# A causal mask folded into the contraction of the decays' matmul, and one projection block moved between its halves

## The reference

```
proj = x @ W_in.T;  gate, (x, B, C), dt = split(proj)
x, B, C = silu(causal_conv4(x, B, C) + conv_b)
dt = softplus(dt + dt_bias);  a = cumsum(dt * A)        # in chunks
L[l, s] = exp(a[l] - a[s]) for s <= l, else 0           # per head
Y = ((C B^T) * L) @ (x * dt)  +  exp(a) * C @ state  +  D * x
state = decay * state + (B * decay * dt)^T @ x
out = rmsnorm_by_group(Y * silu(gate)) * norm_weight @ W_out.T
```

## Time and profile before

| | us |
|---|---|
| median of 3 runs | 3062.11 (3061.02 to 3063.52) |
| profiled execution | 3058.52 |
| its span, first to last instruction | 3056.8 |
| PE busy / DVE / ACT / POOL | 2694.2 / 2116.4 / 1210.2 / 1138.0 |

### The profile page before, as it was taken

How to read it: one execution, slowest core, us unless ns; L and a number is a source line. 1 busy time by engine, 2 the same in 40 slices (tenths; PEclk the granted TensorE clock), 3 DMA queues, 4 the chain that set the end, 5 groups by cost and what they waited for, 6 DMA issues and landing times. The chain is left out here.

```text
span 3056.8 us, 44174 instructions
## 1 busy us (share of the span) xinstructions
PE 2694.2 (88%) x14212; PEld 1934.6 (63%) x14212; DVE 2116.4 (69%) x3433; ACT 1210.2 (40%) x2468; POOL 1138.0 (37%) x1240
## 2 busy tenths in 40 slices
PE   4893399999999999999999993699999959999993
PEld 2782277777777777777777772588888743333332
DVE  3466788888888888888888865677777765444434
ACT  1121255555555545545545541122222234444441
POOL 0350155464555545555455450355455400000000
PEclk9996599999999999999999996799999979999997
DMA  3100200000000000000000001100000031111114
GB/s 114 40 16 29 66 2 2 26 2 26 2 2 26 2 26 2 26 2 2 26 2 3 2 2 55 29 24 29 23 23 29 6 109 36 37 36 38 38 27 93
DMA packets 79209, 82.76 MB, mean 27 GB/s; under 512 B 22043, under 2 KB 67894, under 8 KB 76748
## 3 DMA queue, kind: packets, MB, share of 16 engines
q1 hardware_dynamic: 77516, 80.59, 8.9%
q10 hardware_dynamic: 1536, 0.20, 0.0%
HBM read 61.53 MB, written 16.78 MB: 26 GB/s over the span
## 5 line engine op out<-in xcount | busy, mean ns | idle before, releaser
L731 DVE SCALAR_TENSOR_TENSOR mix_cv<-mix_pp,mix_cw,mix_cv 128x384 f32<-128x384 f32 (+4 forms) x864 | 494.1, 572 | 90.7 <-ACT mix_cv L653 67.6
L1492 DVE TENSOR_REDUCE att_tops<-att_psc 128x1 f32<-128x512 f32 (+3 forms) x384 | 202.2, 555 | 217.9 <-PE att_psc L1430 131.7
L962 POOL TENSOR_TENSOR ffn_hl<-ffn_h,ffn_hh 128x512 fp32r<-128x512 f32 x144 | 186.2, 1293 | 319.8 <-ACT ffn_hh L1020 319.8
L653 ACT ACTIVATE mix_cv<-mix_pp,mix_cb,mix_cw 128x384 f32<-128x384 f32 (+1 forms) x288 | 182.0, 632 | 307.3 <-PE mix_pp L77 305.8
L1467 PE MATMUL att_po<-att_pr,att_vh 128*17 128x512 f32 (+3 forms) x768 | 290.6, 489 | 0.0
L577 PEld LDWEIGHTS mix_pyd<-mix_xdt,mix_lm 128*128 128x128 f32 x2048 | 247.4, 192 | 55.0 <-issue 53.1
L519 POOL TENSOR_TENSOR mix_xdt<-mix_xtok,l_dt 128x512 f32<-128x512 f32 x128 | 133.7, 1044 | 379.0 <-ACT mix_xtok L680 379.0
L1531 ACT ACTIVATE att_pr<-att_pst 128x512 f32<-128x512 f32 (+3 forms) x384 | 175.6, 489 | 249.5 <-PE att_pst L1449 246.0
L75 PE MATMUL mix_pp<-l0in_XH,mix_wx_lo 128*128 128x384 f32 (+2 forms) x576 | 231.0, 401 | 30.9 <-DVE mix_ss L720 21.7
L628 PE MATMUL mix_pgt<-mix_wo,mix_gt 128*128 128x256 f32 x1024 | 251.9, 390 | 2.9 <-issue 2.2
L577 PE MATMUL mix_pyd<-mix_xdt,mix_lm 128*128 128x64 f32 x2048 | 242.7, 272 | 0.9 <-DVE mix_lm L781 0.9
(11 more groups left out here) (296 smaller groups left out, 6753.6 us busy)
## 6 DMA issues: line engine op xcount, KB each, us to landing
mix_w_raw<-in_w_in SPq DMA_DIRECT2D x8, 1280.0 KB, 5.5
ffn_raw<-in_wgu SPq DMA_DIRECT2D x56, 128.0 KB, 2.2
mix_ll<-cs SPq DMA_DIRECT2D x384, 2.0 KB
att_qs<-q SPq DMA_DIRECT2D x192, 32.0 KB
mix_wo_raw<-in_w_out SPq DMA_DIRECT2D x8, 512.0 KB, 7.5
ffn_draw<-in_wd SPq DMA_DIRECT2D x28, 128.0 KB, 2.1
q<-qkv_part SPq DMA_DIRECT2D x24, 128.0 KB, 1.9
k<-qkv_part SPq DMA_DIRECT2D x24, 128.0 KB, 1.9
```

Source lines behind the costliest of these rows:

```text
L653: act.activation(conv_tile(k), pp[k % 2][:, halo:cols], ACT.Identity, bias=cb[:, it // 2, ct:ct + 1], scale=cw[:, it // 2, ct, 3:4]).then_ ...
L731: last = dve.scalar_tensor_tensor(out, of, cw[:, g, ct, 3 - d:4 - d], out, ALU.mult, ALU.add)
L962: pool.tensor_tensor(hl[u % NH][:, :], h[u % 2][:, :], hh[u % NH][:, :].bitcast(F32), ALU.subtract).then_inc(lo_done, 1)
L1492: dve.tensor_reduce(tops[o][:, col:col + 1], psc[g % 2][:, 0:end - c], AX.X, ALU.max).then_inc(mx_done, 1)
```

## The change

The mask becomes part of the first matmul. `ll` and `rl` grow from 27 rows to 96: rows 27 to 31 are zero, and rows 32 to 95 are 64 mask rows. Row 32+r of `rl` has -3e38 at the columns l with l % 64 = r in every head; row 32+r of `ll` has, for token half f, a one where s > r + 64 f. As 64 rows serve only 64 values of l, a half of the decays is done in two matmuls, for l below 64 and from 64 on, each with its own stationary operand (`ll` has now two copies of the a rows beside two sets of mask rows) and 4 x 64 = 256 columns, which are four runs of 64 in `rl` and in `pd`. Both have start and stop set. `identb`, `maskb`, their two casts and the mask's load are gone. The loads of `ll` write each row twice.

In the slot, the last fill now stands ahead of `decays(c, 1)`, not behind it. The other engines' orders stay.

```
-        rl = [s.sb(f"rl{j}", [27, GH, Q], BF16) for j in range(2)]
-        ll = [s.sb(f"ll{j}", [27, Q], BF16) for j in range(2)]
-        maskb, identb = s.sb("maskb", [P, 4 * Q], BF16), s.sb("identb", [P, P], BF16)
+        rl = [s.sb(f"rl{j}", [KD_ROWS, GH, Q], BF16) for j in range(2)]      # KD_ROWS = 32 + 64
+        ll = [s.sb(f"ll{j}", [KD_ROWS, 2, Q], BF16) for j in range(2)]
...
-                        sp.dma_start(ll[c % 2][3 + i * GH:3 + (i + 1) * GH, :],
-                                     cs3[i, g * GH:(g + 1) * GH, at]).then_inc(cs_in[c % 2], 16)
+                        sp.dma_start(ll[c % 2][3 + i * GH:3 + (i + 1) * GH, :, :],
+                                     cs3[i, g * GH:(g + 1) * GH, at].unsqueeze(1).to_broadcast([GH, 2, Q])).then_inc(cs_in[c % 2], 16)
...
-                    pe.matmul(pd[:, :], ll[o][:, :], rl[o][:, 4 * i:4 * i + 4, :], start=True, stop=False)
-                    pe.matmul(pd[:, :], identb[:, :], maskb[:, :], start=False, stop=True).then_inc(d_done, 1)
+                    for f in range(2):
+                        at = slice(f * HQ, (f + 1) * HQ)                     # HQ = 64
+                        last = pe.matmul(pd[:, :].rearrange("p (h q) -> p h q", h=4)[:, :, at], ll[o][:, f, :],
+                                         rl[o][:, 4 * i:4 * i + 4, at], start=True, stop=True)
+                    last.then_inc(d_done, 1)
...
+                    if len(ks) > 1:
+                        fill(ks[-1])
                     if live:
                         decays(c, 1)
-                    if len(ks) > 1:
-                        fill(ks[-1])
...
-                dve.tensor_copy(maskb[:, :], masks_f[:, :]).then_inc(made_v, 1)
-                dve.tensor_copy(identb[:, :], ident[:, :]).then_inc(made_v, 1)
...
+    for r in range(HQ):
+        sel_rows[KM + r, :, r::HQ] = BIG                                     # KM = 32
+        for f in range(2):
+            one_rows[KM + r, f, r + f * HQ + 1:] = 1
```

More of the change, by code:

```diff
@@ L340 @@
 NB18 = NCT * NSEG
+KM, HQ = 32, Q // 2
+KD_ROWS = KM + HQ
 def mixer(nc, w_in, conv_w, conv_b, d_skip, norm_w, w_out, XH, XL, cs3, sel_rows, one_rows,
-          mask4, ident, TE1, TDT, TDTD, DCH, ACC):
+          ident, TE1, TDT, TDTD, DCH, ACC):
     NC = G0 * 2 * CPS
@@ L386, in mixer @@
             s.sem(n) for n in ("xdt_done", "xdtd_done", "xd_done", "t1x_done", "cd_done", "rs_v", "rs_done"))
-        masks_f, rows_f, ones_f = t1[0], y[0], y[1]
+        rows_f, ones_f = (y[0], t1[1]), y[1]
         def place(c):
@@ L446, in _ @@
                 load_weights(0)
[L447 to L450, removed]
+                for i in range(2):
+                    sp.dma_start(rows_f[i][0:KD_ROWS, :], sel_rows[:, i * 512:(i + 1) * 512]).then_inc(const, 16)
+                sp.dma_start(ones_f[0:KD_ROWS, 0:2 * Q], one_rows).then_inc(const, 16)
                 sp.wait_ge(made, 1)
@@ L711, in _ @@
                 dve.memset(ACC[:, :, :], 0.0).then_inc(made_v, 1)
-                dve.wait_ge(const, 64)
-                dve.tensor_copy(maskb[:, :], masks_f[:, :]).then_inc(made_v, 1)
-                dve.tensor_copy(identb[:, :], ident[:, :]).then_inc(made_v, 1)
+                dve.wait_ge(const, 48)
                 for o in range(2):
[L716 to L719, removed]
+                    dve.tensor_copy(ll[o][:, :, :].rearrange("p f s -> p (f s)"), ones_f[0:KD_ROWS, 0:2 * Q]).then_inc(made_v, 1)
+                    for i in range(2):
+                        dve.tensor_copy(rl[o][:, 4 * i:4 * i + 4, :].rearrange("p h l -> p (h l)"),
+                                        rows_f[i][0:KD_ROWS, :]).then_inc(made_v, 1)
+                dve.wait_ge(made_v, 9)
                 dve.memset(ss[0][:, :], 0.0).then_inc(made, 1)
@@ L1685, in build @@
                 mixer(nc, w_in, conv_w, conv_b, d_skip, norm_w, w_out, XH, XL, cs3, c_sel_rows, c_one_rows,
-                      c_mask4, ident, *tabs, X)
+                      ident, *tabs, X)
             with ExitStack() as ctx:
@@ L1730, in lay_out @@
     mask_sl = np.where(k[:, None] > k[None, :], np.float32(BIG), np.float32(0))
-    sel_rows = np.zeros((27, GH, Q), np.float32)
+    sel_rows = np.zeros((KD_ROWS, GH, Q), np.float32)
     for r in range(3 * GH):
         sel_rows[3 + r, r % GH] = -1
-    one_rows = np.zeros((27, Q), np.float32)
+    one_rows = np.zeros((KD_ROWS, 2, Q), np.float32)
     one_rows[:3] = 1
+    for r in range(HQ):
+        sel_rows[KM + r, :, r::HQ] = BIG
+        for f in range(2):
+            one_rows[KM + r, f, r + f * HQ + 1:] = 1
     expert = np.zeros((96, HID1), np.float32)
@@ L1758, in lay_out @@
         c_ident=np.eye(P, dtype=np.float32), c_mask4=c(np.tile(mask_sl, (1, 4))),
-        c_sel_rows=c(sel_rows.reshape(27, -1)), c_one_rows=one_rows, c_h128=had.astype(np.float32), c_expert=expert)
+        c_sel_rows=c(sel_rows.reshape(KD_ROWS, -1)), c_one_rows=c(one_rows.reshape(KD_ROWS, -1)), c_h128=had.astype(np.float32), c_expert=expert)
 def kernel(**inputs):
```

## The result

The changed kernel takes 2949.64 us (median; 2948.61 to 2950.26) against 3061.57 for the kernel before in the same session: ratio 0.9636, 95% interval 0.962 to 0.9653, so 112 us faster. The forecast was 2976. The stated range of 2948 to 3012 holds the time, but only 1.6 us from its lower end, and the forecast's own narrower range, 2955 to 2995, does not. The profiled span went from 3056.8 to 2948.2.

A forecast was written before the change was run, and what follows sets the result against it. TensorE was taken to bound the mixer, VectorE close under it. A pass falls from 90.9 to 85.7 us, 83 us over 16, plus 3 of setup: 2976 us, 2948 to 3012 holding a bit over 8 in 10.

The forecast's parts named there:

- A half costs 0.24, saving 0.40: Decays' matmuls on TensorE: two 256-column matmuls over 96 rows take 0.24 us a half instead of 0.64.
- rival at 3083: Running in 64-column pieces costs TensorE 0.88 us a half, making the kernel slower, 3083 us; chance 0.04.
- rival at 3000: Weight loads of the decays' matmuls are not hidden, each half takes 0.44 us, time 3000 us; chance 0.13.
- The moved fill lets part 1 be cashed: Last fill between the halves, 1.06 us, covers the 0.16 us gap and most of the seam's 1.48.
- part 1: The decays' cheaper matmuls: 0.40 us saved a half, 6.4 us of TensorE per pass of eight slots.
- VectorE's waits before the taps vanish when it is late: In two-fill slots VectorE's 0.77 us wait before the first taps hangs on TensorE and goes when VectorE is late.
- rival of rigid waits: VectorE's 0.77 us wait before the taps stays, its slot would be 11.2 us, time 3011; chance 0.07.
- New waits of 3.4 us a pass: TensorE waits in three-fill slots, the slot after and the seam: 0.8, 0.5, 0.6, 1.4 and 0.1 us.
- Half of the clock's falls stay, 0.5 a pass: Falls of the granted clock after the mixer's seams: half stay, costing 0.5 us a pass.
- rival at 3049: The clock falls at every new wait, 3 falls of 1.7 us a pass, time 3049; chance 0.05.
- Setup, 3 us faster: Ahead of the first fill: two mask casts leave VectorE's path, 3 us gained, bounds 1.5 and 3.5.
- The offset of 3.6 us between profile and median: Median of the runs is 3.6 us above the profiled execution, so the forecast of 2972.5 becomes 2976.

The follow-up runs named there:

- rows96: The kernel before with the decays' operands padded by zero rows from 27 to 96, mask still a second matmul: 3028.81 us, ratio 0.9888.
- mask_only: The changed kernel's new decays matmuls, with the last fill put back behind the second half: 3019.53 us, 0.986 of the kernel before.
- move_only: The kernel before with only the last fill moved ahead of the second half, old decays matmuls kept: 3027.81 us, ratio 0.9885.
- seam_move: The kernel before with the last fill moved only in the 16 seam slots, where the batch turns over: 3029.88 us, ratio 0.989.
- three padded kernels: The kernel before with only the decays' operands padded by zero rows to 96, 33 or 64 rows: 3028.81, 3056.79 and 3050.21 us.
- const_first: The changed kernel with the three constant loads issued ahead of the weights' load: 2948.45 us, 0.9636 of the kernel before.

## Why the prediction was right, and where its sizes were off

1. *A half costs 0.24, saving 0.40*: held. It is 0.22 to 0.23, with no price on entry or exit, and the 64-column pieces cost nothing (rival at 3083). The loads are hidden (rival at 3000): that of the first half starts at 945.72, 0.11 ahead of its matmul, where before it started at 1182.32, 0.01 ahead. rows96 shows that rows 6 had been read rightly.
2. *The moved fill lets part 1 be cashed*: held, and measured: 34 of the 112 us exist only with both, nearly all of them TensorE's wait for ScalarE and not the clock.
3. *VectorE's waits before the taps vanish when it is late*: held, 64.4 us to 4.5; the rival of rigid waits (3011) falls. VectorE's lag in a plain slot is 0.93 to 1.0, against 1.1.
4. *New waits of 3.4 us a pass*: the term that was too large. At a wide three-fill slot 0.62 (0.8 forecast), narrow 0.39 (0.5), the slot after 0.22 (0.6), seam about 1.0 (1.4 and its 0.1 before the output product), plain slots 0: sum 2.25. The places were right; VectorE's work in a three-fill slot is 975.40 - 962.84 = 12.56 and not 12.9. The prediction took off 0.80 of waiting from the slot before the change and missed about 0.3 more: 0.22 before the middle block's taps (start to start 0.69 from 1195.54 to 1196.23 before, 0.47 from 968.69 to 969.16 now), the rest before the first. The leaving lag was 1.5 (wide) and 1.3 (narrow), not 1.6 to 1.7, and the waits behind it are smaller with it. The 3.02 from taps to the seam's second half held (978.11 to 981.12).
5. *Half of the clock's falls stay, 0.5 a pass*: none does after 400 us, until the mixer ends. The clock never fell at the new waits either (rival at 3049). The half rested on a seam wait nearly as long as before, and that wait is 0.9 us. The falls before were also more than read: 7 in the ten seams of the 900 us, not five or six, and the pass that the sum starts from has one in two. Together with 4 that is 3.9 - 2.25 = 1.65 a pass, 26 us over 15.5 passes: the pass was forecast at 85.7 and takes 84.0.
6. *Setup, 3 us faster*: the term that was wrong in sign. The start is 1 us slower. The first fill comes 0.9 earlier (354.81 to 353.93) though the mixer began 0.8 later, but the casts wait for a load that lands late (347.23), and GpSimd's splitting of the weights, which ended at 351.64 before, now ends at 353.47, because its load too landed later (it starts at 346.11 and not 344.73), so that little more could be gained. Then the first product by heads runs at a low clock, 3.67 us for 2.00 before; the prediction has no term for this. A fall at the start shows in mask_only, move_only and seam_move too and in none of the three padded kernels; why stays open. That is 4 us the other way.
7. *The offset of 3.6 us between profile and median*: it belonged to that one execution of the kernel before, whose runs spread by 7 us. The changed kernel's median is at its profiled execution. So 26 for passes, less 4, plus 4 is the miss of 26 us.

So the mechanism in the mixer was right, and the terms mis-sized are the new waits (18 us in all) and the falls (8 us). The prediction had named both as the way to its lower bound, with 15 and 8. That the range holds is in part luck: items 6 and 7 missed by 4 us each, in opposite directions, and with the setup alone as forecast the time would be near 2946, outside it.

## What to carry to other kernels

A cheaper operation ahead of a wait gives only part of its worth until something else is put into the wait: price the two edits together, and expect each alone to give less than its share. When two engines run close under each other, follow the late one's lag from slot to slot. Here the idle time in the late engine's own chain stayed (109.9 us to 111.3), and the idle time that hung on the other engine went (64.4 to 4.5). Then put the extra piece of work where the blocks are smallest. And look at the weight loads: a contraction over few rows between full ones can cost more than the zero rows that would fill it up.

## What the runs showed of the hardware

- Matmuls over 27, 33 and 64 contraction rows between ones over 128 cost 0.10 us on entering and 0.10 on leaving, and the weight loads on either side, 0.09 to 0.10 us, start only with their matmuls. With 96 rows they start 0.10 to 0.21 ahead, and there is no price. Zero rows alone, at the same work, brought 34 us, of which the clock falls that went with them are 16.
- A moving operand and a result in four runs of 64 columns cost nothing over a plain one: two matmuls of 256 columns take 0.22 us, as one of 512 does (rows96, 935.72 to 935.94).
- The granted clock fell after TensorE waits of 1.48 us at 10 of 15 seams in the kernel before, after waits of 1.47 at 10 of 15 with 33 rows and at 4 of 15 with 64, after 2.23 at 11 of 15 in mask_only, and at none of 15 in rows96, where the seam's wait is 2.10. Its windows:

```profile
600.00:1500.00 900.00, 864.35 (x4946) 708.26 (x5027) 760.45 (x1279) 470.97 (x1015) 511.57 (x573) 1.00 0.04 12
```

  So the length of that wait alone does not decide it; what does stays open. Each of these is one profiled execution. A fall costs 1.62 us, with the clock near its 1.2 GHz level for 3.4 us.
- VectorE's cast into `rl` (L720, 96 x 512) took 2.02 us from 347.99, while GpSimd's L503 ran (347.66 to 349.72), in the changed kernel, and 0.41 in const_first, where the same cast starts at 343.87 and GpSimd stands idle until 346.93.
- The kernel before spread from 3056.8 to 3063.5, the changed one from 2948.6 to 2950.3. That fewer falls are the reason is not shown: rows96, without a fall in its mixer, spread from 3023.9 to 3029.5.
